# Moving the first layer's dispatch into its attention, and giving the shared expert a stage of its own

## The reference

```python
x = x + tanh(g_xattn[l]) * attention_l(layernorm(x), ctx)     # 16 heads of 8; layer 0 rotates keys and values (rope)
x = x + tanh(g_ffn[l])   * ffn_l(layernorm(x))
# ffn_0: h = layernorm(x')*gamma + beta, x' the layer-normed input; logits = h @ router_w.T (8 experts)
#        probabilities = softmax; the two best, renormalised; routed experts (SwiGLU, 384 wide) weighted by them
#        plus one shared expert (SwiGLU, 128 wide) for every token
# ffn_1: soft gate, one expert set, dense;  ffn_2: quantised linear layer;  ffn_3: two best of 8 experts, 512 wide
```

## Time and profile before

| | us |
|---|---|
| median of 3 executions (3120.79 to 3130.46) | 3123.79 |
| the profiled execution's own time | 3137.81 |
| its span, first to last instruction | 3135.9 |
| layer 0's attention, up to the first instruction behind barrier 0 | 459.11 |
| layer 0's dispatch, up to the first pad DMA behind barrier 1 | 246.9 |
| mean granted TensorE clock, as a share of full speed | 0.911 |

### The profile page before, as it was taken

How to read it: one execution, slowest core, us unless ns; L and a number is a source line. 1 busy time by engine, 2 the same in 40 slices (tenths; PEclk the granted TensorE clock), 3 DMA queues, 4 the chain that set the end, 5 groups by cost and what they waited for, 6 DMA issues and landing times. The chain is left out here.

```text
span 3135.9 us, 74670 instructions
## 1 busy us (share of the span) xinstructions
PE 2488.7 (79%) x28198; PEld 1774.6 (57%) x28198; DVE 1529.7 (49%) x4205; ACT 1398.1 (45%) x2024; POOL 997.5 (32%) x1066
## 2 busy tenths in 40 slices
PE   4788865537999699989999995988868888178883
PEld 2455443326888455557777773555535555167773
DVE  2555545443444377752222223777747888323332
ACT  2555533222333266655554553555536666034441
POOL 4444434662444212210000000111111355724444
PEclk9999986658999799989999997999979999589997
DMA  3101100115666412210000001111111121156667
GB/s 100 25 21 22 24 18 28 42 42 175 192 196 194 125 46 63 54 25 1 0 0 0 0 0 44 36 38 33 39 29 29 38 57 51 49 175 189 187 189 226
DMA packets 143783, 219.67 MB, mean 70 GB/s; under 512 B 27177, under 2 KB 94513, under 8 KB 143026
## 3 DMA queue, kind: packets, MB, share of 16 engines
q1 hardware_dynamic: 96930, 90.25, 11.2%
q10 hardware_dynamic: 29232, 90.37, 9.2%
q0 software_dynamic: 17408, 36.21, 3.3%
HBM read 157.48 MB, written 43.61 MB: 64 GB/s over the span
## 5 line engine op out<-in xcount | busy, mean ns | idle before, releaser
L1682 DVE TENSOR_REDUCE mx<-psS 128x16 f32<-128x1024 f32 x264 | 322.5, 1222 | 306.7 <-PE psS L1195 305.1
L696 POOL DMA_INDIRECT yg<-ysb,yidx x288 | 279.5, 970 | 418.8 <-DVE ysb L2224 189.7
L800 ACT ACTIVATE work<-psT 128x1024 f32<-128x1024 f32 x260 | 266.3, 1024 | 214.7 <-PE psT L1204 213.4
L794 ACT ACTIVATE work<-work 128x1024 f32<-128x1024 f32 x264 | 278.3, 1054 | 140.9 <-DVE work L1684 135.4
L1195 PE MATMUL psS<-kexp,qT 64*64 64x512 f32 x2112 | 301.3, 643 | 34.4 <-DMA kexp<-kT 23.1
L1684 DVE TENSOR_TENSOR work<-psS,mx 128x1024 f32<-128x1024 f32 x264 | 323.3, 1224 | 9.0
L470 POOL TENSOR_TENSOR ve<-mv,eps 128x4 f32<-128x4 f32 x85 | 17.0, 199 | 965.5 <-DVE mv L1658 963.3
L1204 PEld LDWEIGHTS psT<-ident,work 128*128 128x128 f32 x2080 | 238.1, 145 | 138.2 <-issue 80.3
L1204 PE MATMUL psT<-ident,work 128*128 128x128 f32 x2080 | 286.5, 282 | 2.2 <-ACT work L800 1.6
L1541 PEld LDWEIGHTS psY<-w_ffn,work 128*128 128x128 f32 x2016 | 247.6, 192 | 9.3 <-DVE work L2195 1.2
L1541 PE MATMUL psY<-w_ffn,work 128*128 128x128 f32 x2016 | 248.4, 275 | 1.6 <-DVE ysb L2218 1.0
(11 more groups left out here) (286 smaller groups left out, 4558.3 us busy)
## 6 DMA issues: line engine op xcount, KB each, us to landing
w_ffn<-in_wmoe ACTq DMA_DIRECT2D x72, 578.0 KB, 3.9
w_ffn<-in_wmoe ACTq DMA_DIRECT2D x72, 576.0 KB, 3.8
ctxT<-in_ctxT SPq DMA_DIRECT2D x76, 256.0 KB, 2.7
xin<-xg SPq DMA_DIRECT2D x144, 132.0 KB, 2.8
kexp<-kT SPq DMA_DIRECT2D x1152, 16.0 KB
gio<-yg SPq DMA_DIRECT2D x16, 512.0 KB, 4.0
work<-yg SPq DMA_DIRECT2D x16, 512.0 KB, 6.4
yg<-ysb,yidx POOLq DMA_INDIRECT x288, 3.1
```

Of the source, the lines that this page charges most:

```text
L696: e.indirect_dma_start(out=yg, out_offset=bass.IndirectOffsetOnAxis(ap=yidx[:, b, t:t + 1], axis=0), in_=ysb[:, b, t, :], in_offset=None, ...
L794: e.activation(sc[:, s % 2], sc[:, s % 2], ACT.Exp).then_inc(p_ok, 1)
L800: e.activation(pT[:, s % 2, :], psT[:, :], ACT.Copy).then_inc(pt_ok, 1)
L1682: e.tensor_reduce(mx[:, :], src, AX, ALU.max).then_inc(s_max, 1)
```

## The change

Layer 0 calls `attention_routed(0)` on all five engines where it called `attention(0)`. `dispatch` is deleted, and `shared_expert()` stands between barriers 0 and 1 on PE, ACT and DVE.

- **In the attention.** Layer 0's turns are now written out (the loop register goes). They get the routing of layer 3 with layer 0's 31 steps; the transposed rows are emptied with gamma and beta (`turned`), into a region of w_ffn of their own, and `expo2` is one more ACT operation per group. On POOL `rope_v(u+1)` stands at the start of a turn and `rope_k(u+2)` between the third and the fourth pair of scatters.
- **Placing the values.** `rope_v` ends with one addition in place (128x512) where it had two additions of 64 partitions each; the placing into v2 is now ACT's (`v_place`, two copies of 64 partitions), in step 2 ahead of `k_out`.
- **The last scatters.** POOL enters barrier 0 after the normalisation of chunk 15 and issues its last 24 pairs (48 scatters) behind it, while the other engines compute the shared expert. The block table is computed before barrier 0.
- **The shared expert.** For each of the 16 chunks DVE normalises the rows again from statistics that are now kept for all tiles (mmv, mrstd), PE turns them, ACT empties them, PE computes the two halves, ACT the Silu, DVE the product, PE the product with the down matrix into one of two PSUM tiles in turn, and DVE adds to x. Its weights are loaded to columns 1152 to 1535 of w_ffn.
- **Elsewhere.** The third row buffer lies at the end of w_ffn, so the third weight load of either expert loop waits for the scatters that read it. The statistics of layer 3 wait for the update of x and for the previous statistics, no longer for the rows. Two semaphores that nobody waits for are replaced by another.

```diff
+        ring = [gio[:, 0, :, :], gio[:, 1, :, :], w_ffn[:, 4096 - GT * XW:4096].rearrange(...)]
+        wsh = w_ffn[:, 1152:1536]
+        xTd = {0: w_ffn[:, 1536:2048], 3: v32}
...
@@ rope_v (POOL)
-                e.wait_ge(rope1, val(i, u, 4, 4))
-                if i is not None or u >= 2:
-                    e.wait_ge(pv_ps, val(i, u - 1, LT, K0))
-                for par in range(2):
-                    rows_ = slice(64 * par, 64 * par + 64)
-                    m = e.tensor_tensor(v2[rows_, u % 2, ...], v3(v32[rows_, :], 64), v3(kv_rot[rows_, :], 64), ALU.add)
-                m.then_inc(v_ok, 1)
-                e.wait_ge(v_ok, val(i, u, 1, 1))
+                e.wait_ge(rope1, val(i, u, 5, 4))
+                e.tensor_tensor(v32[:, :], v32[:, :], kv_rot[:, :], ALU.add).then_inc(rope1, 1)
@@ attention_routed (POOL)
                 for u in range(CHUNKS):
+                    if lay == 0:
+                        rope_v(None, u + 1)
                     behind_weighing(u, 0)
...
                     behind_weighing(u, 1)
                     behind_weighing(u, 2)
+                    if lay == 0:
+                        rope_k(None, u + 2)
                     behind_weighing(u, 3)
...
                 norm(CHUNKS - 1)
+                if lay == 0:
+                    barrier(e, 0)
                 for k in range(8 * (NG - 3), 8 * NG):
                     scatter(k)
@@ ACT
+            def v_place(u):
+                e.wait_ge(rope1, 5 * u + 5)
+                if u >= 2:
+                    e.wait_ge(pv_ps, val(None, u - 1, LT, K0))
+                for par in range(2):
+                    rows_ = slice(64 * par, 64 * par + 64)
+                    m = e.activation(v2[rows_, u % 2, ...], v3(v32[rows_, :], 64), ACT.Copy)
+                m.then_inc(v_ok, 1)
...
+                        if s == 2 and inside and lay == 0:
+                            v_place(u + 1)
                         if s == 2 and inside:
                             k_out(lay, None, u + 2)
...
+            def shared_expert():            # ACT
+                def xt_in(c):
+                    e.wait_ge(sh_t, c + 1)
+                    if c >= 2:
+                        e.wait_ge(su_ps, c - 1)
+                    e.activation(xT[:, c % 2, :], psX[:, :], ACT.Identity, bias=vec[:, 7:8], scale=vec[:, 6:7]).then_inc(sh_xt, 1)
+                def silu(c): ...
+                xt_in(0)
+                xt_in(1)
+                for c in range(CHUNKS):
+                    silu(c)
+                    if c + 2 < CHUNKS:
+                        xt_in(c + 2)
@@ PE
+            def shared_expert():
+                def turn_in(c):             # 4 transposes of 128x128 into psX
+                    e.wait_ge(sh_n, c + 1)
+                    if c >= 1:
+                        e.wait_ge(sh_xt, c)
...
+                def up(c):                  # 2 products of 128x512 into psU
...
+                def down(c):                # 4 products of 128x128 into psG[c % 2]
...
+                turn_in(0)
+                turn_in(1)
+                up(0)
+                for c in range(CHUNKS):
+                    if c + 2 < CHUNKS:
+                        turn_in(c + 2)
+                    if c + 1 < CHUNKS:
+                        up(c + 1)
+                    down(c)
@@ DVE
+                rows_in(0)                  # shared_expert: 4 tensor_scalar of 128x128
+                rows_in(1)
+                for c in range(CHUNKS):
+                    if c + 2 < CHUNKS:
+                        rows_in(c + 2)
+                    mul(c)
+                    if c >= 1:
+                        add(c - 1)
+                add(CHUNKS - 1)
...
-            attention(0)
+            attention_routed(0)
+            block_table(0)
             barrier(e, 0)
-            dispatch(0)
-            block_table(0)
+            shared_expert()
             barrier(e, 1)
```

More of the change, by code:

```diff
@@ L392, in experts @@
                 sp.wait_ge(pad_done, 16 * E * (1 + lay // 3))
[L393 to L397, removed]
+                for k in range(4):
+                    sp.wait_ge(m[f"sd{k}"], 16 * 2 * GT * (NG // 4))
                 def rows_in(j):
@@ new lines, in shared_expert, with rows_in, mul, add @@
+            def shared_expert():
+                def rows_in(c):
+                    if c >= 2:
+                        e.wait_ge(sh_t, c - 1)
+                    for t in range(LT):
+                        k = c * LT + t
+                        m = e.tensor_scalar(xnb[c % 2][:, t, :], xs(None, c, t), mmv[:, k, 0:1], mrstd[:, 1, k:k + 1],
+                                            ALU.subtract, ALU.mult)
+                    m.then_inc(sh_n, 1)
+                def mul(c):
+                    e.wait_ge(su_act, c + 1)
+                    if c >= 2:
+                        e.wait_ge(sd_ps, c - 1)
+                    e.tensor_tensor(hbuf[:, c % 2, :], psU[2 * (c % 2) + 1], sg[:, c % 2, :], ALU.mult).then_inc(su_h, 1)
+                def add(c):
+                    e.wait_ge(sd_ps, c + 1)
+                    e.wait_ge(sh_n, c + 1)
+                    e.scalar_tensor_tensor(xs(None, c, 0, LT), psG[c % 2][:, :], tg[:, 4:5], xs(None, c, 0, LT),
+                                           ALU.mult, ALU.add).then_inc(su_x, 1)
+                rows_in(0)
[7 more added lines that the diff above has]
+                add(CHUNKS - 1)
```

327 lines of the change are left out of this document (84 added, 243 removed).

## The result

The changed kernel takes **3018.3 us** (median of 4 runs, 3014.0 to 3022.4) against 3126.3 of the kernel before (4 runs): ratio 0.965, 95% interval 0.9634 to 0.9665. The forecast was 3016, range 2987 to 3066.

A forecast was written before the change was run, and what follows sets the result against it. Layer 0's dispatch was taken as a chain from group to group that no engine fills. Terms -246.9 + 70 + 25 + 43 + 1 = -108 took the median from 3123.8 to 3016 us, range 2987 to 3066.

The forecast's parts named there:

- Old stage gone: Layer 0's separate dispatch stage between barriers 0 and 1 disappears: -246.9 us.
- Tail: End of the routing, through the block table, moves ahead of barrier 0: +25 us.
- Shared expert's stage: New stage between barriers 0 and 1: 70 us, ended by PE's chain, with POOL's scatters to the pads at 65.
- the 4 us for two chunks until the clock is up: Start of the shared expert's stage: PE's first two chunks below full clock add some 4 us.
- the last scatter ending 5 us ahead of DVE: Sign in the shared expert's stage: POOL's last scatter ends 5 us before DVE does.
- Turns: Layer 0's attention turns lengthen: three transitions at 24.4, four at 26.0, eight at 27.3 against quiet 23.5; +43 us.
- POOL's list and the spread as a loop of two turns: Layer 0's attention: POOL's list, key rotation and spread make two turns at least 53.8 us, one 26.9.
- the placing's +0.9: Layer 0's turns: ACT placing values ahead of emptying the keys delays key copy, second projection and next scores by 0.9 us.
- The turns hardly grow: Rival, layer 0's attention: routing's products and scatters fit into waits, +16 instead of +43, 2989 us; 10%.
- POOL as the bound with the scatters on top: Rival, layer 0's attention: POOL bounds the turn, 33.7 us in eight transitions instead of 27.3, 3067 us; 20%.
- Stage at half clock: Rival, shared expert's stage: PE stays at half clock, 126 us instead of 70, 3072 us; 6%.
- Scatters stretched: Rival, attention and shared expert: scatters lengthen beside busy DVE, 3170 us at 3.0 us each, slower than before; 3%.

The follow-up runs named there:

- e4: Changed kernel with POOL going past barrier 0 into its last 48 scatters without waiting for the other engines; 3012.1 us, ratio 0.9632.
- e6: Changed kernel with POOL's last 48 scatters issued ahead of barrier 0, so the shared expert runs without them; 3055.9 us, ratio 0.9775.
- e9: Changed kernel with ACT's placing of the values between the two copies of the keys instead of ahead of both; 3006.2 us, ratio 0.9621.
- e16: e9 plus DVE's normalising of the router's rows moved to the end of a turn's third step, beside scatters; 3005.2 us, ratio 0.9612.
- e10: e9 plus e3 on the changed kernel: placing between the keys' copies and keys' rotation ahead of the third scatter pair; 2984.6 us, ratio 0.9561.
- e3: Changed kernel with the keys' rotation on POOL ahead of the third pair of scatters instead of behind it; 3017.9 us, ratio 0.9666.

## Why the prediction was right

- **Old stage gone, -246.9:** as read.
- **Tail, +25:** +24.1, right. POOL did reach the barrier long before DVE (21.46 us of idle time), and by e4 that wait cost 9 us. The forecast named the wait but priced its effect at nothing, since it had PE end the stage.
- **Shared expert's stage, 70, PE's chain to end it:** the size was near (67.1), the engine wrong, and that the size was met is luck: PE's chain was overpriced by 13 us, and POOL's list, forecast at 65, stood just below the 70. A chunk costs PE 3.05 us (the two rows below, 13 chunks apart), not 3.4: I added durations, and matmuls of one group start before the modelled end of the group ahead. That is 5.6 us in 16 chunks. The other 7 lie in the front and the end of the stage; the 4 us for two chunks until the clock is up are shown by no run, since the clock was 1.00 from the first product with the down matrix on (531.00). So DVE ends 56.1 us behind the stage's start (57.2 with the 1.1 to the pads in e4), and POOL's 48 scatters (61.3, from 521.42 to 582.75) with 5.05 to the pads end the stage. Of the signs that the forecast named, "the last scatter ending 5 us ahead of DVE" failed: it ended 6.0 us behind DVE. e4 and e6 show both sides.

```profile
531.00 1.05 PE L1431 MATMUL psO<-w_ffn,work 128*128 128x128 f32 x8
570.61 1.05 PE L1431 MATMUL psY<-w_ffn,work 128*128 128x128 f32 x8
```

- **Turns, +43:** +37.4. 27.3 was forecast for the eight transitions with scatters, and the last eight measure 27.0. The three early ones at 24.4 were 26.8, 24.6 and 25.3, the four at 26.0 were 26.9, 26.2, 25.3, 26.9: these seven sum to 181.9 against 177.2. All 15 took 398.3 us where the forecast's lengths add to 395.6. That the difference still came out 5.7 below +43 lies in what it was set against: the profile of before averages 24.1 a turn, 8.4 us above 15 turns of the quiet 23.5, and I took the difference from quiet turns.
- **The mechanism, POOL's list and the spread as a loop of two turns:** borne out by e9 and e16 (opening the other limits changes nothing) and by e10 (shortening the list does, once the copy is in time). What I missed is that the placing's +0.9, counted as a small delay, makes a limit of its own as high as the loop's: with it in place, 2.5 us less on POOL's list brought nothing (e3).
- **Rivals.** The turns hardly grow (+16): no, +37.4. POOL as the bound with the scatters on top (33.7 a turn): no; with the same number of scatters e10 has 24.8. Stage at half clock: no, 0.86, and 1.00 once it ran. Scatters stretched: no, median 0.975 us, longest 1.252 of 256, also beside the 64 normalisations (single ones reached 1.47 in e4 and 1.49 in e6). The rule of the Trainium skill (SBUF — State Buffer, Who interferes with whom) that GpSimd's descriptors starve beside them would have made, by the estimate in the forecast, 149 us of the stage's scatters; they took 61.3. What did show is the other side: in e9 DVE's four normalisations took 4.53 us in place of 1.11 and ended 0.6 us behind POOL's rotation. The trace agrees there with the same section of the Trainium skill, by which of a DVE instruction and a GpSimd one that want the shared ports one waits for the whole of the other.
- **Profile and median.** The forecast's -108 was made on a profile that lies above its median; on the profiles the change was -123.7, on the medians -108.0. That the median was met within 3 us is partly luck: the terms were 15.7 us short, and the two profiles lay 11.5 us above and 4.3 below their medians, 15.8 together, which cancels it.

## What to carry over

A wait that vanishes without a gain can mean a second limit at the same height: look in the new trace for what is late now, and try the two edits together before dropping either. A placement or a copy put ahead of another copy on a helping engine is priced by who waits behind it, here TensorE, whose clock can fall in the gap and add to what it costs. Where two engines share a stage, count the slower one from when it may start: an engine that idles at a barrier for work that needs no barrier gives the idle time away.

## What was not expected of the hardware

- TensorE ran on at the lower clock behind gaps of 1.8 to 3.3 us between its instructions, but not behind every such gap: it kept the full clock behind 1.84 us in the changed kernel's turn (287.57), and behind 2.82 us in e16's (273.18, scores in 1.09 us), and had the lower one behind 1.84 us in e3's (292.29). What else decides was not isolated.
- VectorE's four normalisations took 1.11 us beside scatters (e16) and up to 5.06 beside GpSimd's rotation (e9).
- On one of the four chips that the experiments ran on ScalarE and VectorE stood for up to 31.6 and 20.4 us, released by nothing on the core. Whether the changed kernel would have had these stops there was not measured.
